# Moving a softmax coefficient to GpSimd, the difference half a head later, and two-part fp16 scores, in a differential-attention block with a ternary feed-forward part

## What is computed

```
q, k, v = hs @ Wq.T, hs @ Wk.T, hs @ Wv.T      # 32 query parts, 16 key parts of 16 columns, 8 values of 32
q, k = rope(q), rope(k);  q = q * 16 ** -0.5   # keys and values are shared by 2 heads
scores = q @ k.T + causal                      # 16 heads x 2 parts
probs = softmax(scores)
diff = probs[:, :, 0] - lambda_full * probs[:, :, 1]
attn = diff @ v                                # then an RMS norm per head, * subln_weight, * (1 - LAMBDA_INIT)
x = x + attn @ Wo.T
h = gelu(layernorm(x) @ ternary(w1).T + b1)    # 512 -> 2048
x = x + h @ ternary(w2).T + b2
```

## Time and profile before

| | us |
|---|---|
| median of 3 runs | 4374.92 (4374.47 to 4382.02) |
| the profiled execution's own time | 4370.7 |
| its span in the trace | 4368.9 |
| busy: PE, DVE, ACT, POOL | 3625.1, 3369.0, 2913.5, 1495.9 |
| batch 4 (first exponential to first exponential) | 529.1 |

### The profile page before, as it was taken

The page is one execution under the profiler, slowest core; times in us unless marked ns, Lnnn a source line. Parts: engine busy times, 40 slices in busy tenths (PEclk is TensorE's granted clock), DMA queues, the critical chain, the costliest instruction groups (busy, mean ns, idle before and its releaser), DMA issues.

```text
span 4368.9 us, 81035 instructions
## 1 busy us (share of the span) xinstructions
PE 3625.1 (83%) x23454; PEld 2157.1 (49%) x23454; DVE 3369.0 (77%) x6188; ACT 2913.5 (67%) x6786; POOL 1495.9 (34%) x1563
## 2 busy tenths in 40 slices
PE   2688888888888888888888988888888888888886
PEld 1345554455445454554545545555545555554553
DVE  6778967888678886788767887678877788678881
ACT  1567766777567775677756766667666777567772
POOL 0243234332333334332343324433134432333323
PEclk7788999989899899998889988999989989899998
DMA  4212112211122112212122110222122111222110
GB/s 133 54 25 41 24 43 43 40 23 33 35 43 43 23 38 46 43 25 38 26 43 43 36 31 23 47 37 43 25 44 43 32 31 25 44 43 43 20 37 14
DMA packets 146768, 166.71 MB, mean 38 GB/s; under 512 B 16640, under 2 KB 117632, under 8 KB 145792
## 3 DMA queue, kind: packets, MB, share of 16 engines
q1 hardware_dynamic: 146304, 161.13, 18.3%
HBM read 105.95 MB, written 55.12 MB: 37 GB/s over the span
## 4 chain that ended last, share of the span: by engine, by line
PE 41%; DVE 25%; issue 19%; ACT 8%; DMA 3%; SPq 2%; POOL 1%; DVEq 1%; ACTq 1%; POOLq 0%
DVE NM L667 9%; PE M L822 7%; PE M L872 7%; PE SP_ L837 6%; PE F L894 6%; PE DP L849 5%; PE F L907 4%; DVE E L691 3%; ACT E L543 3%; DVE CC L688 2%; DMA KST<-scratch 2%; PE M L816 2%; DVE NM L675 2%; PE SP_ L838 1%; PE DX L849 1%
## 5 line engine op out<-in xcount | busy, mean ns | idle before, releaser
L543 ACT ACTIVATE E<-SP_,NM 128x256 f32<-128x256 f32 (+7 forms) x2048 | 1518.3, 743 | 674.7 <-DVE NM L667 461.8
L667 DVE TENSOR_REDUCE NM<-SP_ 128x1 f32<-128x896 f32 (+3 forms) x1024 | 1034.2, 1018 | 257.8 <-PE SP_ L838 254.0
L837 PE MATMUL SP_<-KST,QST 96*128 96x512 bf16 (+3 forms) x3072 | 866.2, 356 | 394.5 <-ACT E L543 329.5
L691 DVE SCALAR_TENSOR_TENSOR E<-E,CC 128x512 f32<-128x512 f32 (+7 forms) x1024 | 928.6, 907 | 36.2
L555 ACT ACTIVATE DT<-DP 128x512 f32<-128x512 f32 (+3 forms) x1024 | 527.7, 515 | 534.9 <-PE DP L849 501.5
L849 PE MATMUL DP<-ident,E 128*128 128x128 f32 x3328 | 617.5, 304 | 140.4 <-DVE E L691 136.7
L675 DVE TENSOR_REDUCE NM<-SP_ 128x2 f32<-128x1024 f32 (+3 forms) x512 | 420.2, 821 | 309.2 <-PE SP_ L838 306.5
L837 PEld LDWEIGHTS SP_<-KST,QST 96*128 96x128 bf16 x3072 | 278.9, 103 | 745.7 <-ACT E L543 515.0
L894 PE MATMUL F<-X2H,W1Q 128*128 128x256 f16 x2048 | 512.1, 287 | 71.0 <-ACT HP L598 67.0
L849 PEld LDWEIGHTS DP<-ident,E 128*128 128x128 f32 x3328 | 395.6, 154 | 313.9 <-issue 164.3
L822 PE MATMUL M<-WQKV,WT 128*128 128x512 f32 x1040 | 531.7, 608 | 8.8 <-DVE T L650 4.1
(11 more groups left out here) (87 smaller groups left out, 4794.6 us busy)
## 6 DMA issues: line engine op xcount, KB each, us to landing
QST<-scratch SPq DMA_DIRECT2D x390, 128.0 KB, 4.4
scratch<-SPL SPq DMA_DIRECT2D x65, 576.0 KB, 2.8
KST<-scratch SPq DMA_DIRECT2D x390, 64.0 KB, 4.8
X<-in_x SPq DMA_DIRECT2D x66, 256.0 KB, 3.3
out<-SQ SPq DMA_DIRECT2D x64, 256.0 KB, 2.0
KST<-in_w1T SPq DMA_DIRECT2D x1, 4096.0 KB, 19.4
DT<-in_w2T SPq DMA_DIRECT2D x1, 4096.0 KB, 28.8
WQKV<-in_wqT SPq DMA_DIRECT2D x1, 1024.0 KB, 6.9
```

Source lines behind the costliest of these rows:

```text
L543: act.activation(dst, score_out(i, 2 * n + k, w), ACT.Exp, bias=NM[:, (2 * u + k) % 8:(2 * u + k) % 8 + 1], scale=1.0, accum_out=SUM[:, i ...
L667: nc.vector.tensor_reduce(NM[:, m:m + 1], score_out(i, 2 * n + k, P * (i + 1)), AX.X, ALU.max, negate=True).then_inc(max_ready, 1)
L691: nc.vector.scalar_tensor_tensor(out=E1[:, u % 2, 0:w], in0=E2[:, e:e + w], scalar=CC[:, u % 2:u % 2 + 1], in1=E1[:, u % 2, 0:w], op0=ALU. ...
L837: pe.matmul(SP_[:, k[a // 512], 0:n], q, KST[0:ROWS, a // P:(a + n) // P, kk, :], start=True, stop=not last)
```

## The change

- The coefficient moves from DVE to POOL (`ratio`): a power of -1 with a tensor of -1 in place of the reciprocal, then the same tensor_scalar. It stands at the start of an even half-head, before POOL's other items, for the head before; `R2` and `CC` get four columns.
- The difference of head n-1 moves on DVE from half-head 2n to 2n+1, which for t >= 4 is behind both row maxima of head n. Transposes move from 2n+1 to 2n+2, the copies to `DT` and the products with the values likewise.
- `E1` has 4 rows and `E2` 2 rows (before 2 rows, and 1 row or two halves).
- Most fixed places move one half-head later, `LN1_TURN` two; `SPLIT_AT`, `GELU`, `W1_AT`, `W2_AT` and `OUT_AT` stay.
- Scores take two fp16 parts: high, and the rest times 64, with high/64 as the third stored part, so that three products of 16 rows do. The two key groups of a head's stack lie on rows 0 to 47 and 48 to 95 of one `KST` column, which has half the columns, and the query's rows of the other group stay zero. POOL's `split` becomes two tensor_scalars without a wait between. `stack` still issues 6 + 6 copies, of half the size.
- The weights w1 are loaded in four pieces to `KST`, `HH` and `HL`, and both sums of |w| take four reductions.

The core of the diff:

```diff
-PROD = 6
-QPART = (0, 0, 0, 1, 1, 2)
-KPART = (0, 1, 2, 0, 1, 0)
-ROWS = PROD * DH
+PROD = 3
+QPART = (0, 2, 1)
+KPART = (0, 1, 2)
+PART = PROD * DH
+ROWS = 2 * PART
+LOW = 64.0
...
-LN1_STATS, LN1_ROWS, LN1_TURN = 1, 3, 4
-Q_PROJ, Q_ROPE = (7, 8, 9, 10), 11
-KV_PROJ, KV_ROPE = (12, 13, 14, 14), 15
-Q_TURN, Q_REST, K_TURN, K_REST = 16, 17, 20, 21
-V0_MOVE = 5
-PV_OUT = (19, 3)
-SUM_INVERSE, AT_TURN, AT_ROWS = 5, 6, 6
-MEAN_SQ, RMS_ROWS, AN_TURN = 9, 13, 22
-O_PROJ, O_SUM = (23, 24, 25, 26), 27
-LN2_STATS, LN2_ROWS, LN2_TURN, LN2_REST = 27, 29, 30, 31
+LN1_STATS, LN1_ROWS, LN1_TURN = 1, 3, 6
+Q_PROJ, Q_ROPE = (8, 9, 10, 11), 12
+KV_PROJ, KV_ROPE = (13, 14, 15, 15), 16
+Q_TURN, Q_REST, K_TURN, K_REST = 17, 18, 21, 22
+V0_MOVE = 6
+PV_OUT = (20, 4)
+SUM_INVERSE, AT_TURN, AT_ROWS = 5, 7, 7
+MEAN_SQ, RMS_ROWS, AN_TURN = 10, 14, 23
+O_PROJ, O_SUM = (24, 25, 26, 27), 28
+LN2_STATS, LN2_ROWS, LN2_TURN, LN2_REST = 28, 30, 31, 31
...
 # SP, stack(): the same for KST with source columns 4 + a
-                for j in range(PROD):
-                    sp.dma_start(QST[DH * j:DH * (j + 1), tile % 2, :, :].rearrange("p (s c) n -> p s c n", s=8),
-                                 src[QPART[j], :, :, 0:4, :]).then_inc(stacked, 16)
+                for a in range(2):
+                    for j in range(PROD):
+                        r = PART * a + DH * j
+                        sp.dma_start(QST[r:r + DH, tile % 2, :, :].rearrange("p (s c) n -> p s c n", s=8)[:, :, 2 * a:2 * a + 2, :],
+                                     src[QPART[j], :, :, 2 * a:2 * a + 2, :]).then_inc(stacked, 16)
...
 # POOL
-                pool.tensor_scalar(SPL[:, 1, c], T2[:, c], 1.0, 0.0, ALU.mult, ALU.add).then_inc(mid_part, 1)
-                after(pool, mid_part, 2 * nb + part + 1)
-                pool.tensor_tensor(SPL[:, 2, c], T2[:, c], SPL[:, 1, c], ALU.subtract).then_inc(split_done, 1)
+                pool.tensor_scalar(SPL[:, 1, c], T2[:, c], LOW, 0.0, ALU.mult, ALU.add)
+                pool.tensor_scalar(SPL[:, 2, c], SPL[:, 0, c], 1.0 / LOW, 0.0, ALU.mult, ALU.add).then_inc(split_done, 1)
...
+            def ratio(b, i, n):
+                u = i * H + n
+                gu = b * N_U + u
+                col = 8 * (n // 8) + 4 * (n % 2) + (n % 8) // 2
+                c = slice(u % 4, u % 4 + 1)
+                hold(pool, exp_done, 2 * gu + 2)
+                pool.tensor_tensor(R2[:, c], SUM[:, i % 2, 1, col:col + 1], minus1[:, :], ALU.pow).then_inc(inverse_out, 1)
+                hold(pool, d_ready, gu - 3)
+                hold(pool, inverse_out, gu + 1)
+                pool.tensor_scalar(CC[:, c], R2[:, c], SUM[:, i % 2, 0, col:col + 1], neglam[:, 0:1], ALU.mult,
+                                   ALU.mult).then_inc(ratio_ready, 1)
...
                 for hs in range(HS_TILE):
+                    s, h = divmod(hs, 2)
+                    if h == 0 and T.before(s - 1):
+                        ratio(*T.before(s - 1))
...
 # ACT
-                    old = T.before(s - 1) if h else T.before(s - 2)
+                    old = T.before(s - 2)
...
-                    if old and (h == 1 or groups(old[1]) == 2):
-                        dt_copy(*old, 1 - h)
+                    if old and (h == 0 or groups(old[1]) == 2):
+                        dt_copy(*old, h)
...
 # DVE, diff()
-                after(dve, exp_done, 2 * gu + 2)
-                nc.vector.reciprocal(R2[:, u % 2:u % 2 + 1], SUM[:, i % 2, 1, col:col + 1]).then_inc(d_chain, 1)
-                after(dve, d_chain, 2 * gu + 1)
-                nc.vector.tensor_scalar(CC[:, u % 2:u % 2 + 1], R2[:, u % 2:u % 2 + 1], SUM[:, i % 2, 0, col:col + 1],
-                                        neglam[:, 0:1], ALU.mult, ALU.mult).then_inc(d_chain, 1)
-                after(dve, d_chain, 2 * gu + 2)
+                after(dve, ratio_ready, gu + 1)
...
-                    if h == 0 and T.before(s - 1):
+                    if h == 1 and T.before(s - 1):
                         diff(*T.before(s - 1))
...
 # PE
-                    if h == 1:
-                        if T.before(s - 1):
-                            for g in range(groups(T.before(s - 1)[1])):
-                                diff_transposes(*T.before(s - 1), g)
-                        half_v(T, s, 1)
+                    if h == 0:
+                        if T.before(s - 2):
+                            for g in range(groups(T.before(s - 2)[1])):
+                                diff_transposes(*T.before(s - 2), g)
+                        half_v(T, s - 3, 1)
```

More of the change, by code:

```diff
@@ L375, in stack @@
             def stack(nb, tile, q_free, k_free):
-                hold(sp, stacked, 16 * 2 * PROD * (nb - 1))
+                hold(sp, stacked, 64 * PROD * (nb - 1))
                 hold(sp, split_done, 2 * nb + 2)
@@ L382, in stack @@
                 hold(sp, s_ready, q_free)
-                for j in range(PROD):
-                    sp.dma_start(QST[DH * j:DH * (j + 1), tile % 2, :, :].rearrange("p (s c) n -> p s c n", s=8),
-                                 src[QPART[j], :, :, 0:4, :]).then_inc(stacked, 16)
+                for a in range(2):
[3 more added lines that the diff above has]
+                                     src[QPART[j], :, :, 2 * a:2 * a + 2, :]).then_inc(stacked, 16)
                 if k_free is not None:
                     hold(sp, s_ready, k_free)
-                for j in range(PROD):
-                    sp.dma_start(KST[DH * j:DH * (j + 1), tile, :, :].rearrange("p (s c) n -> p s c n", s=8),
-                                 src[KPART[j], :, :, 4:6, :]).then_inc(stacked, 16)
+                for a in range(2):
+                    for j in range(PROD):
+                        r = PART * a + DH * j
+                        sp.dma_start(KST[r:r + DH, tile, :, :], src[KPART[j], :, :, 4 + a, :]).then_inc(stacked, 16)
             def result(T, j):
@@ L418, in _ @@
             sp.wait_ge(x_in[1], 16 * (B * TILES // 2 + 1))
-            sp.wait_ge(stacked, 16 * 2 * PROD * (B * TILES + 1))
+            sp.wait_ge(stacked, 64 * PROD * (B * TILES + 1))
         @block.gpsimd
@@ L508, in _ @@
             split(0, 1)
+            pool.wait_ge(ready, 3)
             every_block(pool, pool_work)
@@ L531, in exp @@
                 if k == 0:
-                    old = T.before(n - 2)
+                    old = T.before(n - 4)
                     if old:
@@ L535, in exp @@
                         after(act, t_ready, pb * N_T + tg(pi, pn, groups(pi) - 1) + 1)
-                    dst = E1[:, u % 2, 0:w]
+                    dst = E1[:, u % 4, 0:w]
                 else:
-                    after(act, d_ready, b * N_U + u - (1 if i < 4 and u > 0 else 0))
-                    e = 512 * (u % 2) if i < 4 else 0
-                    dst = E2[:, e:e + w]
+                    after(act, d_ready, b * N_U + u - 1)
+                    dst = E2[:, u % 2, 0:w]
                 col = 8 * (n // 8) + 4 * (n % 2) + (n % 8) // 2
@@ L829, in scores @@
                 if s == 0:
-                    after(pe, stacked, 16 * 2 * PROD * (b * TILES + i + 1))
+                    after(pe, stacked, 64 * PROD * (b * TILES + i + 1))
                 after(pe, exp_done, b * N_E + SLOT_FREE[i * NQ + s])
                 q = QST[0:ROWS, i % 2, (s % 8) * 4 + s // 8, :]
-                kk = ((s // 2) % 8) * 2 + (s // 2) // 8
+                kk = (s // 2) % 8
                 for a in range(0, w, 512):
```

61 lines of the change are left out of this document (35 added, 26 removed).

## The result

The changed kernel took 4530.98 us (median, 4526.36 to 4538.13) against 4374.69: a ratio of 1.0357, with a 95% interval of 1.0344 to 1.0370. The forecast of 4295 and both of its ranges (4200 to 4360, and 4130 to 4450 for eight in ten) are missed, on the wrong side. The case that came nearest is the rival called "POOL's bursts decide", which had been given 4455, 4384 to 4520, and a chance of 0.25; the measured time lies 11 us above even its upper end.

The account below looks back on a forecast made before the run. DVE's order was taken to bound wide tiles, hand-overs between engines the narrow ones. Tile terms summed to -9.7 us a batch, -78 over eight, forecasting 4295 us; likeliest 4200 to 4360, eight in ten 4130 to 4450.

Parts of the forecast that it names:

- POOL's bursts decide: Rival: DVE waits at heads 8, 9, 14, 15 of odd tiles; slower, about 4455 us (4384 to 4520); chance 0.25.
- relief: Work taken off DVE: 0.50 us a head, 192 us off the present chain, 510 us as ceiling.
- the bursts: Odd tiles: four hidden-layer splits on POOL after each GELU, 2.65 us each, delay coefficients and so DVE's difference.
- 16 x 0.5 = 8 us where DVE rules and a bit more for the order: Wide tiles: DVE's saving per tile, taken as -6, -4.5, -9 and -4 us for tiles 4 to 7.
- The term for the second burst: After odd tiles' second GELU, head 14's coefficient comes late: +6.1, +5.6, +4.4 us in tiles 1, 3, 5; tile 7 nothing.
- the first burst: After odd tiles' first GELU, coefficients of heads 8 and 9 wait: +1.9 and +1.3 us in tiles 1 and 3.
- I estimate 24.0 us between the two GELUs: Tile 1: DVE catches up after late coefficients, 24.0 us where there were 22.1, so +1.9.
- the coefficient's price: One coefficient on POOL, power, wait and tensor_scalar: about 0.95 us per head, range 0.85 to 1.15.
- collisions: DVE's two-input difference and POOL's SBUF reads exclude each other; expected mostly to miss, nothing taken; costly-collision rival had chance 0.04.
- the slower rival: Same as "POOL's bursts decide": slower once even tiles give less than the 20 us the bursts take; chance 0.25.
- issue time and latency rule the 12, so I take nothing: Half-size stack copies: no gain, bounds -1 and +1 us for each of two places in a batch that wait.
- the first rival: Full relief comes through, bursts absorbed: about 4040 us, or 4125 with half the burst cost left; chance 0.20.

Follow-up runs that it names:

- e10: Kernel before with only the two-part fp16 scores and their smaller stacks, exponential rows still 2 and 1; 4319.0 us.
- e1: Changed kernel with the coefficient back on DVE, everything else as changed; 4361.97 us.
- e6: Changed kernel with coefficient on DVE and the old places, difference, transposes, copies and products; fp16 scores and 4 and 2 rows stay; 4312.5 us.
- e2: Changed kernel with the coefficient left out, the difference taking minus lambda as its factor (a ceiling, not a usable kernel); 4283 us.
- e3: Kernel before with the coefficient left out, the difference taking minus lambda as its factor (a ceiling, not a usable kernel); 4235 us.
- e11: e6 with the changed kernel's later fixed places, difference, transposes and copies staying half a head earlier; 4599.5 us.
- e14: Changed kernel with the coefficient on POOL for heads of even tiles only, on DVE for those of odd tiles; 4378 us.
- e12: e6 with HS = 1 in place of 1/16, so each piece of POOL's hidden split takes two instructions, not three; 4338 us.
- e9: Changed kernel with each hidden-split instruction on POOL cut to 16 of 512 columns, the rest left zero; 4291 us.

## Why the prediction was wrong

**The account.** From before to the changed kernel: fp16 scores -56 (e10), rows -6, new order with the coefficient on DVE +49 (e1 less e6), the coefficient on POOL +169 (changed less e1): +156. By tile, 0 to 7, the batch became longer by -0.2, +10.8, +0.3, +9.6, -1.6, +7.1, -6.4 and +1.5 us, together +21.1, where the prediction's sum has -9.7. By the run without a coefficient (e2), 18.7 of these 30.8 us are relief that did not come, and by 12.1 POOL's coefficient cost more than the bursts had been put at.

**The relief was over-sized.** The prediction's terms without the bursts come to -29 us a batch (1, 1, 2, 1.5, 6, 4.5, 9, 4). Leaving the coefficient out of the changed kernel altogether gives -10.3 (526.9 to 516.6), the scores' gain of about 5 included. The step that failed is "16 x 0.5 = 8 us where DVE rules and a bit more for the order", drawn from a busy share of 86 to 89%. It held for tile 6 alone (8.1 us in e3). In tile 4, with almost the same share, e3 gave 1.2, and the chain had said so: PE's lines. Over all tiles e3 gave 18.3 a batch. "A bit more for the order" is wrong in its sign: the order cost 49 us with the coefficient on DVE and 85 without one.

**The bursts were under-sized, by the first one.** The term for the second burst was 6.1, 5.6 and 4.4 us for tiles 1, 3 and 5, and nothing for tile 7. Over batches 1 to 6, the stretch from the second GELU to the next tile's first exponential grew by 6.3, 6.1, 4.9 and 2.2. So close a match is in part luck. With the coefficient on DVE (e1) the stretch had already grown by 1.2, 0.9, 2.9 and 2.4; POOL's coefficient added 5.1, 5.2, 2.0 and nothing. The sum from rows was right for tiles 1 and 3 to within 1 us, and too high for tile 5. For the first burst +1.9 and +1.3 had been taken for tiles 1 and 3, "I estimate 24.0 us between the two GELUs", and nothing for 5 and 7. That stretch grew by 4.7, 4.2, 4.1 and 2.6 in the four odd tiles, and against e1 by 5.2, 4.2, 3.2 and 0.4. The coefficients were only little later than forecast (in tile 1 of batch 4 those of heads 8 and 9 at 11.3 and 16.4 us after the GELU, forecast 10.6 and 15.5); what failed is the catch-up assumed behind them, and that wide tiles would have slack. Ahead of the first GELU tiles 1 and 3 are longer than in e1 by another 2.2 and 1.4, for which the sum had no term. Together the bursts were put at 19.3 us a batch; POOL's coefficient cost 31.4 against none at all (548.0 less 516.6) and 22.3 against one on DVE.

**Right:** the coefficient's price to 0.2 us; POOL's and DVE's busy times; that the rows bring nothing that can be told from noise; the bursts as the place of most of the loss; that collisions add next to nothing (the difference took 917 ns in the mean, 907 before). That transposes and copies half a head later bring nothing by themselves was not tried alone. The deciding point of the slower rival, even tiles giving less than 20 us, is what came: they gave 7.9.

**Wrong, too:** "issue time and latency rule the 12, so I take nothing" for the copies of half the bytes. Scores and copies together are the only part of the change that pays, 56 us; 20 of them are PE's shorter wait for the copies. Two smaller slips stand in the sums: a coefficient of 1.05 us in place of 0.95 is 0.1 us more for each one that waits, not 0.2, and the first rival halves a burst cost of 22 us where the forecast's own terms give 19.3. Neither moves the forecast.

**Open:** what the coefficient's own 1.13 us cost in the new order, apart from the bursts; what e11's 287 us consist of; tile 1 in e14; the part of the scores' gain beyond PE's wait for the stacks; the 0.6% between e6 and e12.

## What to carry to other kernels

An idle share does not say that an in-order engine is free for work on a short loop: list what stands ahead of the new instruction in its queue, with the longest burst, and compare that with the time at which the result is needed. An engine's busy share in a stretch does not say what can be won there. Here the chain of the same stretch was the better guide: it gave the coefficient's tensor_scalar (L688) 1.8% of tile 4, where leaving the coefficient out gave 1.2 us, and L688 and the reciprocal (L686) together 6.8% of tile 6, where it gave 8.1. Leaving the work out, once, gives the ceiling before anything is moved (here 3.2%). And measure the parts of a bundled change alone: this one held 1.3% of gain in the part that seemed neutral, and lost it to the rest.

## What was not expected of the hardware

- A copy from DRAM to 16 partitions landed in 1.9 us with 32 KB and in 4.8 with 64 KB, 2.4 with 64 KB (queries, after) and 4.4 with 128 KB (queries, before), with as many copies and nearly the same packets (146,768 and 146,816 in all): its size showed, though the 12 copies are issued one behind the other.
- POOL's tensor_scalar of one column with two scalars read from memory took 347 ns in the mean; one of 16 columns with constants took 241 to 260 in e9.
- PE's mean granted clock (1.0 is 2.4 GHz, 0.5 is 1.2) was 0.83 in tile 1 of the changed kernel, where PE waited more, and 0.88 before; in tiles 0, 4 and 6 it was 0.94 or 0.95 against 0.89 to 0.92.
